# Shared-expert units, WKV units and layer ends rearranged in a four-layer mixture-of-experts kernel

## The reference

```
f    = side input, same for all layers
cond = sigmoid(x) * num/den * (0.8 + 0.2*tf)      # num, den: decaying sums over time, both ways, of exp(f)*f and exp(f)
L0:  48 experts of width 96, top 8, capacity 96
L1:  8 experts of width 176, top 2, softmax gates;  plus a shared expert of width 352
L2:  14 experts of width 176, top 2;                plus a shared expert of width 352
L3:  16 experts of width 128, top 2, 4-bit weights: w = (q - 8) * block_scale * global_scale
expert, shared:  (silu(c @ wg) * (c @ wu)) @ wd          L3:  relu(c @ w_up)**2 @ w_down
x = x + sum of gate * expert(c) + shared(c)
```

## Time and profile before

| | |
|---|---|
| median of 3 runs | 630.23 us (630.2 to 631.54) |
| profiled execution | 632.02 us, its span 630.2 us |
| busy in the span | PE 502.8 us (80%), PEld 337.1 (53%), DVE 395.4 (63%), POOL 285.3 (45%), ACT 218.2 (35%) |
| chain that ended last, by engine | PE 68%, DVE 11%, issue 7%, DMA 5%, ACT 4%, another core or an unknown queue 2%, POOL 2% |
| mean granted TensorE clock | 0.869 of full |

### The profile page before, as it was taken

The page is one execution under the profiler, slowest core; times in us unless marked ns, Lnnn a source line. Parts: engine busy times, 40 slices in busy tenths (PEclk is TensorE's granted clock), DMA queues, the critical chain, the costliest instruction groups (busy, mean ns, idle before and its releaser), DMA issues.

```text
span 630.2 us, 9033 instructions
## 1 busy us (share of the span) xinstructions
PE 502.8 (80%) x2760; PEld 337.1 (53%) x2760; DVE 395.4 (63%) x805; ACT 218.2 (35%) x555; POOL 285.3 (45%) x259
## 2 busy tenths in 40 slices
PE   1867745899999998998888969898989961967754
PEld 1554533687878776455555454455656461433324
DVE  6887793999999996477672775577621765000003
ACT  2412142222222224145554340355444340333332
POOL 4105306979999720336653002366665003366540
PEclk9778756999999996999999978999999965577796
DMA  8400012999864301736664499365232413889825
GB/s 229 88 2 33 0 34 67 243 239 236 221 164 138 95 1 63 191 101 220 200 183 147 150 291 235 86 212 169 79 90 68 142 45 108 258 270 271 237 86 198
DMA packets 84928, 92.80 MB, mean 147 GB/s; under 512 B 8370, under 2 KB 64274, under 8 KB 84882
## 3 DMA queue, kind: packets, MB, share of 16 engines
q1 hardware_dynamic: 75858, 67.56, 37.7%
q0 software_dynamic: 9024, 24.65, 13.4%
HBM read 72.79 MB, written 19.40 MB: 146 GB/s over the span
## 4 chain that ended last, share of the span: by engine, by line
PE 68%; DVE 11%; issue 7%; DMA 5%; ACT 4%; another core or an unknown queue 2%; POOL 2%; DVEq 0%; SPq 0%; POOLq 0%; ACTq 0%
PE y_ps L647 9%; PE g_ps L777 7%; PE g_ps L741 5%; PE u_ps L741 5%; PE u_ps L620 5%; PE r_ps L724 4%; PE u_ps L693 4%; PE y_ps L530 4%; PE g_ps L702 3%; PE y_ps L711 3%; PE g_ps L782 2%; PE r_ps L762 2%; PE g_ps L635 2%; DMA xg<-ctab,idx 2%
## 5 line engine op out<-in xcount | busy, mean ns | idle before, releaser
L1734 POOL DMA_INDIRECT xs<-ctab,idx_g x76 | 75.6, 995 | 141.2 <-DVE idx_g L1371 70.4
L1741 POOL DMA_INDIRECT ybuf<-o_s,idx_s x76 | 76.3, 1004 | 89.1 <-ACT o_s L964 70.6
L1702 POOL DMA_INDIRECT xg<-ctab,idx x36 | 54.5, 1514 | 36.3 <-DVE idx L1514 28.8
L647 PE MATMUL y_ps<-P,o_hi 128*128 128x512 f32 x144 | 59.7, 414 | 0.2 <-DVE o_lo L1539 0.2
L724 PE MATMUL r_ps<-ident_s,xs 128*128 128x128 f32 x152 | 34.3, 311 | 29.7 <-ACT hT_s L957 13.8
L647 PE MATMUL y_ps<-P,o_lo 128*128 128x512 f32 x144 | 56.6, 393 | 0.0
L1395 DVE TENSOR_TENSOR h_s<-a_s 128x128 f32<-128x128 f32 x24 | 7.1, 297 | 69.8 <-ACT a_s L950 33.6
L724 PEld LDWEIGHTS r_ps<-ident_s,xs 128*128 128x128 f32 x152 | 18.5, 152 | 54.7 <-issue 44.8
L964 ACT ACTIVATE o_s<-g_ps 128x256 f32<-128x256 f32 x76 | 29.1, 383 | 48.8 <-PE g_ps L777 22.9
L942 ACT ACTIVATE xT_s<-r_ps 128x256 f32<-128x256 f32 x76 | 28.8, 379 | 38.3 <-PE r_ps L724 34.6
L620 PE MATMUL u_ps<-xT_g,wup 128*96 128x96 f32 x384 | 37.8, 253 | 0.7 <-DVE hT L1533 0.7
(11 more groups left out here) (265 smaller groups left out, 1112.7 us busy)
## 6 DMA issues: line engine op xcount, KB each, us to landing
wR<-w SPq DMA_DIRECT2D x48, 256.0 KB
wup<-in_wglu SPq DMA_DIRECT2D x36, 256.0 KB
ysb<-ybuf SPq DMA_DIRECT2D x6, 1024.0 KB, 6.7
wR<-in_wglu SPq DMA_DIRECT2D x4, 1216.0 KB
wdn<-in_wglu SPq DMA_DIRECT2D x12, 384.0 KB
raw_q<-in_wq SPq DMA_DIRECT2D x16, 256.0 KB
w<-w3o SPq DMA_DIRECT2D x16, 256.0 KB
ctab<-ysb SPq DMA_DIRECT2D x6, 512.0 KB, 3.1
```

The costliest lines, as they stand in the source:

```text
L647: mm = pe.matmul(y_ps[:, m, hf, :], o[:, b, m * P:(m + 1) * P], P1[:, b, hf * HALF:(hf + 1) * HALF], start=first and n == 0, stop=last and ...
L1702: pool.indirect_dma_start(out=xg[:, j % XG, :], out_offset=None, in_=ctab, in_offset=bass.IndirectOffsetOnAxis(ap=idx[:, j:j + 1], axis=0) ...
L1734: pool.indirect_dma_start(out=xs[:, n % XB, :], out_offset=None, in_=ctab, in_offset=bass.IndirectOffsetOnAxis(ap=idx_g[:, b:b + 1], axis= ...
L1741: pool.indirect_dma_start(out=ybuf, out_offset=bass.IndirectOffsetOnAxis(ap=idx_s[:, b:b + 1], axis=0), in_=o_s[:, n % OB, :], in_offset=N ...
```

## The change

1. **Head of layers 1 and 2.** `shared_gate(0)` moves ahead of `positions2`; both matmul groups of units 0 and 1 and the gate of unit 2 stand between `positions2` and `lists2`; behind `lists2` stand `shared_up(2)` and the three `shared_down`. Each of the first three units gets its own PSUM banks (`bank_gate`, `bank_up`), so that PE needn't wait for ACT and DVE between them. `act_sh` and `h_sh` get three buffers.
2. **WKV units.** Layer 1 keeps five units in its blocks and loses the sixth, which ran beside the shared units behind the blocks. Layer 2 does seven, all in its first 28 blocks.
3. **Layer ends.** PE does `final(0)` ahead of the last `shared_down`, and `final(1)` behind it. ACT and DVE follow: half 0 is weighed, then the last shared unit's silu and product, then half 1. In layers 1 and 2 `add_y(0)` and `cond(0)` follow the weighing of half 1; in layer 3 `add_y(0)` stands ahead of it.
4. **Layer 3's global scales.** `scale_w3` is gone: `unpack` writes `w3o` itself (and waits until the store from two experts ago has landed). The scales come in at layer 3's `block_act` and `block_out` as a per-partition operand.

```diff
-Q0 = [0, UNITS + NGR, UNITS + NGR + 6]
-QN = [0, 6, 6]
+Q0 = [0, UNITS + NGR, UNITS + NGR + 5]
+QN = [0, 5, 7]
...
+        def bank_gate(k):
+            return y_ps[:, 1, 1, :] if k == 1 else u_ps[:, :]
+
+        def bank_up(k):
+            return (y_ps[:, 0, 1, :], g_ps[:, 0, :], g_ps[:, 1, :])[k] if k < SHEAD else g_ps[:, 0, :]
...
                 if k == 0:
                     pe.wait_ge(wsh_in, 16 * SHQ[layer])
-                    pe.wait_ge(ctok_ready, 4 * layer + 4)
-                if k == SHEAD:
+                    wait(pe, sha_ready, n)
+                elif k == 2:
+                    pe.wait_ge(sha_ready, n - 1)
+                elif k == SHEAD:
                     pe.wait_ge(bh_ready, B0[layer] + BK[layer])
-                wait(pe, sha_ready, gk_)
+                elif k > SHEAD:
+                    pe.wait_ge(sha_ready, n)
...
-                wait(pe, shh_ready, gk_)
+                if k == 1:
+                    pe.wait_ge(ctok_ready, 4 * layer + 4)
+                elif k > SHEAD:
+                    pe.wait_ge(shh_ready, n)
...
+                if shared:
+                    shared_gate(layer, 0)
                 positions2(layer)
                 if shared:
-                    shared_gate(layer, 0)
                     shared_up(layer, 0)
                     shared_gate(layer, 1)
+                    shared_up(layer, 1)
+                    shared_gate(layer, 2)
                 lists2(layer)
                 if shared:
-                    shared_up(layer, 1)
-                    shared_down(layer, 0)
-                    shared_down(layer, 1)
-                    shared_gate(layer, 2)
                     shared_up(layer, 2)
-                    shared_down(layer, 2)
+                    for k in range(SHEAD):
+                        shared_down(layer, k)
...
+                final(layer, 0)
+                if shared:
                     shared_down(layer, NSH - 1)
-                for hf in range(2):
-                    final(layer, hf)
+                final(layer, 1)
...
+                    act.activation(a_s[:, n % 2, 0:I3], bank2(n)[:, 0:I3], ACT.Relu, scale=gsc[:, 0:1]
+                                   ).then_inc(ba_ready, 1)
...
-                act.activation(o_s[:, n % OB, :], g_ps[:, 1, n % 2 * C:(n % 2 + 1) * C], ACT.Copy
-                               ).then_inc(o_ready, 1)
+                act.activation(o_s[:, n % OB, :], g_ps[:, 1, n % 2 * C:(n % 2 + 1) * C], ACT.Copy,
+                               scale=gsc[:, 1:2] if layer == 3 else 1.0).then_inc(o_ready, 1)
...
-            def scale_w3(e):
-                act.wait_ge(deq_ready, e + 1)
-                wait(act, w3_in[e % 2], 16 * (e // 2))
-                for k in range(2):
-                    cols = slice(k * C, (k + 1) * C)
-                    ins = act.activation(w3o[:, e % 2, cols], raw_s[:, e % 2, cols], ACT.Copy,
-                                         scale=gsc[:, k:k + 1])
-                ins.then_inc(w3o_ready, 1)
...
                 if shared:
-                    for k in range(SHEAD, NSH):
+                    for k in range(SHEAD, NSH - 1):
                         shared_silu(layer, k)
                 for i in range(TT):
+                    if shared and i == TH:
+                        shared_silu(layer, NSH - 1)
                     weigh_first(layer, i)
...
-                dve.scalar_tensor_tensor(out=raw_s[:, s, :], in0=raw_q[:, s, :], scalar=-8.0, in1=raw_s[:, s, :],
-                                         op0=ALU.add, op1=ALU.mult).then_inc(deq_ready, 1)
+                wait(dve, w3_in[s], 16 * (e // 2))
+                dve.scalar_tensor_tensor(out=w3o[:, s, :], in0=raw_q[:, s, :], scalar=-8.0, in1=raw_s[:, s, :],
+                                         op0=ALU.add, op1=ALU.mult).then_inc(w3o_ready, 1)
...
-                    if layer < 3 and b < 4 * (QN[layer] - 1):
+                    if layer < 3 and b < 4 * QN[layer]:
                         wkv_part(Q0[layer] + b // 4, b % 4)
...
                 if shared:
-                    q = Q0[layer] + QN[layer] - 1
-                    for k in range(SHEAD, NSH):
+                    for k in range(SHEAD, NSH - 1):
                         shared_product(layer, k)
-                        for ph in range(2 * (k - SHEAD), min(2 * (k - SHEAD) + 2, 4)):
-                            wkv_part(q, ph)
-                for i in range(TT):
+                for i in range(TH):
                     weigh_second(layer, i)
-                for hf in range(2):
-                    add_y(layer, hf)
-                    if layer < NL - 1:
-                        cond(layer + 1, hf)
+                if shared:
+                    shared_product(layer, NSH - 1)
+                else:
+                    add_y(layer, 0)
+                for i in range(TH, TT):
+                    weigh_second(layer, i)
+                if shared:
+                    add_y(layer, 0)
+                    cond(layer + 1, 0)
+                add_y(layer, 1)
+                if shared:
+                    cond(layer + 1, 1)
```

More of the change, by code:

```diff
@@ L62 @@
 assert RL[3] >= 3 * UNITS
[L65 to L66 removed]
+Q0 = [0, UNITS + NGR, UNITS + NGR + 5]
+QN = [0, 5, 7]
 DQ = [0, 10, 6]
[L68 removed]
+assert Q0[2] + QN[2] == NL * UNITS and 4 * QN[1] <= BK[1] and 4 * QN[2] <= BK[2]
 assert sum(DQ) == E3 and 2 * DQ[1] <= BK[1] and 2 * DQ[2] <= BK[2]
@@ L204, in build @@
         ctok2 = ysb[:, :, 0:C]
-        act_sh = sb("act_sh", [P, 2, HALF])
-        h_sh = sb("h_sh", [P, 2, HALF])
+        act_sh = sb("act_sh", [P, 3, HALF])
+        h_sh = sb("h_sh", [P, 3, HALF])
         raw_q = sb("raw_q", [P, 2, 2 * C], I32)
@@ L243, in build @@
         idx_s = sb("idx_s", [P, BM], I32)
-        sb("rest", [P, 2 * TT * P])
+        sb("rest", [P, 2 * TT * P - 2 * HALF])
         wR = sb("wR", [P, RW])
@@ L710, in shared_down @@
                 for c in range(KT):
-                    mm = pe.matmul(y_ps[:, c, hf, :], wsd[0:m, j, c * P:(c + 1) * P], h_sh[0:m, k % 2, :],
+                    mm = pe.matmul(y_ps[:, c, hf, :], wsd[0:m, j, c * P:(c + 1) * P], h_sh[0:m, k % 3, :],
                                    start=j == 0, stop=False, skip_group_check=True)
@@ L931, in shared_silu @@
                 act.wait_ge(shg_done, n + 1)
-                wait(act, shh_ready, n - 1)
-                act.activation(act_sh[0:m, k % 2, :], u_ps[0:m, :], ACT.Silu).then_inc(sha_ready, 1)
+                wait(act, shh_ready, n - 2)
+                act.activation(act_sh[0:m, k % 3, :], bank_gate(k)[0:m, :], ACT.Silu).then_inc(sha_ready, 1)
             def bank2(n):
@@ L948, in block_act @@
                 wait(act, bh_ready, n - 1)
-                m, f = (I1, ACT.Silu) if layer < 3 else (I3, ACT.Relu)
-                act.activation(a_s[:, n % 2, 0:m], bank2(n)[:, 0:m], f).then_inc(ba_ready, 1)
+                if layer < 3:
+                    act.activation(a_s[:, n % 2, 0:I1], bank2(n)[:, 0:I1], ACT.Silu).then_inc(ba_ready, 1)
+                else:
+                    act.activation(a_s[:, n % 2, 0:I3], bank2(n)[:, 0:I3], ACT.Relu, scale=gsc[:, 0:1]
+                                   ).then_inc(ba_ready, 1)
             def move_h(layer, b):
@@ L1095, in _ @@
                         block_out(layer, b - 1)
-                    e = unpacked(layer, b - 1)
-                    if e is not None:
-                        scale_w3(e)
                 block_out(layer, BK[layer] - 1)
                 if shared:
-                    for k in range(SHEAD, NSH):
+                    for k in range(SHEAD, NSH - 1):
                         shared_silu(layer, k)
                 for i in range(TT):
+                    if shared and i == TH:
+                        shared_silu(layer, NSH - 1)
                     weigh_first(layer, i)
@@ L1380, in shared_product @@
                 dve.wait_ge(shu_done, n + 1)
-                wait(dve, shd_done, n - 1)
-                dve.tensor_tensor(h_sh[0:m, k % 2, :], act_sh[0:m, k % 2, :], g_ps[0:m, 0, :], ALU.mult
+                wait(dve, shd_done, n - 2)
+                dve.tensor_tensor(h_sh[0:m, k % 3, :], act_sh[0:m, k % 3, :], bank_up(k)[0:m, :], ALU.mult
                                   ).then_inc(shh_ready, 1)
```

13 lines of the change are left out of this document (7 added, 6 removed).

## The result

The changed kernel took 634.72 us (median of 9 executions, 632.85 to 639.96) against 630.23 for the kernel before (9 executions, 625.02 to 637.02): a ratio of 1.0084, 95% interval 1.0051 to 1.0116. It is slower, by 5.3 us by that ratio and by 4.5 us by the medians. On another chip it was measured again and came to 1.0152 (1.0097 to 1.0206; medians 645.64 against 637.49). The forecast was 625.0, its range 618 to 631. A ratio here leaves out executions that took over 1.5% longer than the fastest of their kernel, which flatters a kernel whose times scatter widely, so where it leaves out many, the medians of all executions stand beside it and count for more.

What follows compares the result with a forecast made beforehand. PE was taken as the bound (chain ends on it 68% of the time, mean granted clock 0.869). Terms -1.3 - 3.6 - 1.8 - 0.8 + 0.3 - 0.8 + 0.6 + 2.2 = -5.2 from 630.2 gave 625.0 us, range 618 to 631.

Steps and rivals of the forecast that it cites:

- Head of layer 1: Layer 1 before its blocks: own banks remove PE stalls of 0.46 and 0.84 us, the later gather stays hidden: -1.3 us.
- Head of layer 2: Layer 2 before its blocks: PE's gap becomes a wait for the gather, gain 2.4 us less 0.6 for clock: -1.8 us.
- The clock's cost: Layer 2's first block_up after PE's idle time: 1.2 us slower, counted at even odds as 0.6 us.
- Scales: Blocks of layers 1 and 2 without scale_w3: block_out's distance shrinks, -3.6 us in layer 1, -0.8 us in layer 2.
- The operand's price in layer 3: Layer 3's blocks: ACT's copy with a per-partition scale takes 0.09 us longer, about seven times on the path: +0.6 us.
- Layers' ends: End of layer 2: the second add_y no longer waits behind half 0's work: -0.8 us; layer 1's share counted in layer 2's start.
- Layer 3's end: After layer 3's blocks: add_y(0) ahead of weighing half 1 makes PE wait between the halves of final: +2.2 us.
- full cost of `scale_w3`: Rival, blocks of layers 1 and 2: all 16 scale_w3 cost their whole 0.90 us, gain 14.4 us, total 615.0; chance 0.12.
- "no gain": Rival, blocks of layers 1 and 2: scatter's landing and POOL set the pace, blocks gain nothing, total 629.4; chance 0.20.
- The WKV parts: Layer 2's blocks 20 to 27: eight parts more fit into DVE's room, only POOL's DMA issues slow: +0.3 us.
- a full lock: Rival, layer 2's blocks with WKV: DVE and POOL can't overlap on their shared port, 8.2 us more, total 633.2; chance 0.02.
- the slower rival: Rival, layer 2's first blocks: after PE's wait TensorE stays at 1.2 GHz for 16 us, losing 6.8 us, total 631.8; chance 0.09.

Runs made afterwards that it cites:

- the three orders: Changed kernel with positions2 ahead of shared_gate(0), last shared_down ahead of final(0), layer 3's add_y(0) behind all weighing: 1.0034 of the kernel before.
- the fillers: Changed kernel with matmuls nobody reads behind shared_down(2), 3 in layer 1 and 8 in layer 2: 1.0065 of the kernel before; with 7 and 16: 1.0226.

## Why the prediction was wrong

**Head of layer 1, the step that failed.** "Gather 1 lands near 267.6 here ... the gather stays hidden by 0.9 us." The landing of 5.8 us was read in layer 2 and carried over to a head where a load of 1.4 MB of weights was still under way. PE's wait for the first gather ends 8.2 to 9.1 us after its start there; with that load moved, the rows are there by 5.64.

The 5.8 us were no landing in layer 2 either. The window of the count ended at 398, and seven packets came behind it: 89 of the 288 had moved at 394.5, not 96. And the packets of several gathers move side by side, so 96 of them need not be those of the first two: in the changed kernel's layer 2 PE's wait ended after 6.98 us, when 167 of the 288 had moved. The trace of the kernel before held the warning, though PE came too late there (10.2 us after the first gather) to wait. These are plain loads (q1) and gathers (q0) in the 5.8 us behind the first gather's start, in layer 1 and then in layer 2:

```profile
q1 hardware_dynamic: 853, 0.87, 76.9%
q0 software_dynamic: 47, 0.13, 9.2%
...
q1 hardware_dynamic: 721, 0.73, 67.6%
q0 software_dynamic: 89, 0.27, 19.3%
```

In the head where the 1.3 us were to be gained, 47 of the 288 gather packets had moved, about half as many. So the 1.3 us of stalls turned into a wait, the delay of the first gather that I had called hidden came through (22.1 us behind layer 0's end in the changed kernel, 19.7 before; `block_turn(0)` 30.9 and 29.9: means of six and five), and the clock cost 1.2 us more in the mean (8.9 against 7.8 us from `block_turn` to the first out). Forecast -1.3, measured +2.3.

**Head of layer 2.** The place of the first gather was right: 23.7 + 1.9 + 0.8 = 26.4 us behind the second `add_y` by my steps, 25.9 to 27.6 in five profiles. Its landing was too short again, 6.98 us in the first profile, and `block_turn(1)` came 1.21 us behind `block_turn(0)`, which waits for a gather too; my sum let only `block_turn(1)` wait. So it came 8.2 us behind the first gather, not 5.8. The clock's cost, 1.2 us at even odds, came in all five profiles: 1.5 us from `block_turn(1)` to the first out in the first. Forecast -1.8 with the layer's end, measured +1.5 - 0.5.

**Scales.** Right in sign and kind, with `block_out`'s distance as the loop: -3.6 and -0.8 forecast, -2.3 and -1.1 in the profiles, 0.9963 timed. The standard errors of these two means are 0.7 and 0.8 us. Twelve outs took 38.21 us rather than 37, and in the means of all profiles the same twelve took 40.9 with `scale_w3` and 39.9 without; 3.07 was read from three outs, too few for a stage that scatters so much. The operand's price in layer 3 shows in the row (473 ns against 382) and not in layer 3's blocks.

**Layers' ends.** -0.8 each (layer 1's inside its sum for layer 2's head): measured -0.5 and -0.8. Layer 3's end: +2.2 forecast, 2.5 in the first profile's rows, +2.7 in the means. Right.

**The rivals.** Neither full cost of `scale_w3` nor "no gain" held. The WKV parts are hidden: by my sum a full lock would have made the eight blocks 8 us longer, and 0.6 us is what the table has, within the scatter. The Trainium skill states the lock ("SBUF — State Buffer", "Who interferes with whom"); these blocks don't show such a price. The clock was the slower rival, and I had it in the wrong form: not a long spell at 1.2 GHz but one or two slow blocks at the end of a head, in layer 2 in all five profiles, in layer 1 in four of six. (Its 6.8 us are 6.9 by its own product.) What was missing among the rivals is the plain one, that both heads end with the gathers and PE's savings become idle time.

Open remains whether the timed executions lose more than the profiles' stages show: 5.3 us against 2.4, the latter with a standard error of 1.6. That the loss hangs on the three orders is shown by 1.0152 against 1.0034 on one chip. That part 1 holds its share of it is shown in layer 1's head; in the whole time it isn't, because the run without part 1 scatters too much. The timed gain from the fillers isn't clear of the scatter either.

## What to carry to other kernels

Before counting a saved stall, find what the engine waits for next, and whether that event hangs on the same engine: in a head that ends with a transfer, faster cover work only becomes idle time, and an idle TensorE can pay again in the first block. Cover work that stands ahead of what starts the transfer, here `lists2`, delays the transfer too. A transfer's duration holds only beside the traffic it was read in; look at what else is in the queues at that time, and take as its landing the end of somebody's wait for it, not a count of packets. If cover work ends too early, move the transfer (its queue, the loads beside it), not the cover: here that shortened both heads, if not clearly the whole kernel.

## What the runs showed of the hardware

A gather of 128 rows, with others behind it, was there at the latest 5.6 us after its start where the plain loads moved 0.02 MB or nothing in that time, 6.2 to 7.2 us after it beside 0.6 to 0.8 MB, and 8.2 to 9.5 us after it beside 0.9 to 1.1 MB (counted over 9 us). The issue of a DMA took longer behind large loads: two stores that take 2.39 us to issue took 5.63 when they came directly behind 5 MB of loads, and a small load that took 3.95 us there took 0.56 behind the stores. And in layer 2 eight `pe.matmul` that nobody reads (16 recorded, 7.03 us) kept the granted clock at 1.00 and brought `block_up` from 2.59 to 1.45 us.
